# Routing weights of an expert layer: spread by products on TensorE, or stored to DRAM and read back as broadcast rows

## The reference, cut to what matters

```python
def block(x, c, ...):                        # x: (4, 1024, 256), fp32
    sa, ca, ga, sb, cb, gb = modulation(silu(c) @ wmod)
    h = layernorm(x) * (1 + ca) + sa
    x = x + ga * rwkv(h)                     # token mixing, K/V/R products, scan over T, output product
    h = layernorm(x) * (1 + cb) + sb
    x = x + gb * ffn(h)
    return x

def ffn(x):                                  # 8 experts of width 64, the best 2 are taken, one shared of 128
    logits = x @ gate_w.T
    topk_vals, topk_idx = top_k(logits, 2)
    w = softmax(topk_vals)
    comb = zeros(n, 8).at[arange(n)[:, None], topk_idx].add(w)
    g, u = einsum('nh,ehm->enm', x, Wg), einsum('nh,ehm->enm', x, Wu)
    eo = einsum('enm,emh->enh', silu(g) * u, Wd)
    return einsum('ne,enh->nh', comb, eo) + silu(x @ sWg) * (x @ sWu) @ sWd
```

## Time and profile before

| | us |
|---|---|
| time, median of 3 runs | 409.97 (407.69 to 410.45) |
| the profiled execution | 408.2 |
| its span in the trace | 406.3 |
| TensorE busy in the span | 366.6 |
| VectorE busy | 334.6 |
| ScalarE busy | 295.2 |
| GpSimd busy | 44.7 |

### The profile page before, as it was taken

One profiled execution on the slowest core, in us unless ns is written; L12 is line 12 of the kernel. 1 busy time (PEld: TensorE's weight loads), 2 busy tenths in 40 slices (PEclk: granted clock), 3 DMA queues, 4 the chain that ended last, 5 costly groups with the idle time before them and its releaser, 6 DMA issues.

```text
span 406.3 us, 4276 instructions
## 1 busy us (share of the span) xinstructions
PE 366.6 (90%) x1348; PEld 224.8 (55%) x1348; DVE 334.6 (82%) x667; ACT 295.2 (73%) x466; POOL 44.7 (11%) x76
## 2 busy tenths in 40 slices
PE   4892873999999999999999999999999999969985
PEld 4561332756565845675476646574567455725752
DVE  4799989987989898999899898989898988541541
ACT  2699699846997589948994799759985894324332
POOL 4030013001400050002200230005000200010000
PEclk9995795799999999999999999999999999969999
DMA  8900010001000110011000300011001000100011
GB/s 287 268 5 1 0 52 0 0 2 52 0 2 0 52 52 2 0 52 54 0 2 2 103 0 0 2 53 50 2 1 52 2 0 0 52 2 0 0 53 52
DMA packets 15626, 13.27 MB, mean 33 GB/s; under 512 B 4690, under 2 KB 15092, under 8 KB 15604
## 3 DMA queue, kind: packets, MB, share of 16 engines
q1 hardware_dynamic: 15572, 12.99, 10.4%
q10 hardware_dynamic: 32, 0.01, 0.0%
HBM read 8.80 MB, written 4.19 MB: 32 GB/s over the span
## 4 chain that ended last, share of the span: by engine, by line
PE 63%; ACT 22%; DVE 9%; issue 3%; DMA 1%; SPq 0%; DVEq 0%; ACTq 0%
PE mm L737 29%; PE mm L632 10%; PE yo L765 7%; PE yo L650 7%; ACT arg L391 6%; ACT n_xn L326 5%; PE yo L659 3%; ACT arg L417 3%; ACT pool_x L366 2%; ACT h_h L365 2%; ACT kv L374 2%; DVE h_l L979 2%; ACT arg L405 1%; PE cb L749 1%; DVE mixed L879 1%
## 5 line engine op out<-in xcount | busy, mean ns | idle before, releaser
L632 PE MATMUL mm<-mixed,WT 128*128 128x512 f32 x192 | 87.5, 604 | 8.1 <-DVE mixed L879 8.1
L765 PE MATMUL yo<-act,w_dn 128*128 128x512 f32 x160 | 74.1, 613 | 5.4 <-DVE act L1056 5.4
L632 PEld LDWEIGHTS mm<-mixed,WT 128*128 128x128 f32 x192 | 36.3, 193 | 53.4 <-issue 39.6
L737 PE MATMUL mm<-h_h,w_up_h 128*128 128x512 f32 x160 | 55.2, 426 | 4.3 <-DVE h_l L979 4.3
L765 PEld LDWEIGHTS yo<-act,w_dn 128*128 128x128 f32 x160 | 30.8, 197 | 41.9 <-issue 35.6
L737 PE MATMUL mm<-h_l,w_up_h 128*128 128x512 f32 x160 | 51.1, 401 | 0.0
L737 PE MATMUL mm<-h_h,w_up_l 128*128 128x512 f32 x160 | 51.0, 400 | 0.0
L300 POOL TENSOR_TENSOR n_ve<-n_mv,small 128x4 f32<-128x4 f32 x16 | 8.2, 510 | 310.9 <-DVE n_mv L868 310.9
L374 ACT ACTIVATE kv<-mm,cols 128x512 f32<-128x512 f32 x32 | 21.8, 682 | 18.9 <-PE mm L632 18.9
L737 PEld LDWEIGHTS mm<-h_h,w_up_h 128*128 128x128 f32 x160 | 28.4, 192 | 12.6 <-DVE h_l L979 6.4
L737 PEld LDWEIGHTS mm<-h_h,w_up_l 128*128 128x128 f32 x160 | 30.6, 191 | 7.5
(11 more groups left out here) (149 smaller groups left out, 662.6 us busy)
## 6 DMA issues: line engine op xcount, KB each, us to landing
x_in<-in_L_attn_x_dram SPq DMA_DIRECT2D x8, 512.0 KB, 3.5
out_dram<-pool_x SPq DMA_DIRECT2D x5, 512.0 KB, 2.9
pool_x<-in_L_wmod_dram SPq DMA_DIRECT2D x2, 512.0 KB, 4.9
out_dram<-x_third SPq DMA_DIRECT2D x2, 512.0 KB, 2.9
pool_x<-in_L_wmod_dram SPq DMA_DIRECT2D x2, 256.0 KB, 4.0
pool_g<-in_L_ffn_Wg_dram SPq DMA_DIRECT2D x2, 256.0 KB, 5.0
pool_g<-in_L_ffn_Wu_dram SPq DMA_DIRECT2D x2, 256.0 KB, 4.4
w_dn<-in_L_ffn_Wd_dram SPq DMA_DIRECT2D x1, 512.0 KB, 3.9
```

The source lines that it names most:

```text
L632: last = nc.tensor.matmul(mm[PROJECT_BANK[j]][:, :], WT[:, w, kc, oc * P:(oc + 1) * P], mixed[:, w, kc, :], start=(kc == 0), stop=(kc == K ...
L737: last = nc.tensor.matmul(mm[UP_BANK[i]][:, :], w[:, kc, gu, e * P:(e + 1) * P], rhs[:, kc, :], start=(n == 0), stop=(n == 3 * KH - 1))
L765: last = nc.tensor.matmul(yo[oc][:, :], w_dn[:, e, oc * P:(oc + 1) * P], act[:, e, :], start=(e == 0), stop=(e == NB - 1))
```

## The change

`comb` keeps the eight weights as fp32, without the split in a rounded part and a rest, so `route` has 17 instructions. `turn_comb` turns 8 columns and `comb_out` writes `combT`, now 8 partitions by 512 tokens. The four spread products, their matrix `sel` and its preparation at the start on GpSimd and VectorE are gone. SyncE stores `combT` (16 KB) to a DRAM tensor, waits for that store, and issues eight loads for the chunk: for each block i and each half e of the partitions one DRAM row of 512 weights, read 64 times, into `weights`, a new SBUF tile (128 KB for each load, 1 MB for each chunk). In SyncE's list this `spread(n)` stands ahead of store(n-1) and load(n+3). `weigh` reads `weights` in place of PSUM and waits for the two loads of its block. Weigh 1 and 2 are moved in VectorE's list from before and after gate_up 2 and 3 to behind gate_up 4. `comb_out` also waits for the store of the chunk before, and `turn2` waits for combT_done where it waited for act_done.

```diff
@@ -48,6 +48,8 @@
     x_chunks = x.rearrange("b (g t p) h -> (b g) p t h", t=TT, p=P)
     out_chunks = out.rearrange("b (g t p) h -> (b g) p t h", t=TT, p=P)
 
+    comb_dram = nc.dram_tensor("comb_dram", (E, CH), F32, kind="Internal").ap()
+
     with ExitStack() as ctx:
         def sb(name, shape, dt=F32):
             return ctx.enter_context(nc.sbuf_tensor(name, shape, dt))
...
@@ -99,8 +100,9 @@
         h2_l = sb("h2_l", [P, KH, CH], F32R)
         rt = sb("rt", [P, 8, TT, E])
         r1 = sb("r1", [P, 7, TT])
-        comb = sb("comb", [P, TT, 2 * E], F32R)
-        combT = sb("combT", [P, CH], F32R)
+        comb = sb("comb", [P, TT, E])
+        combT = sb("combT", [E, CH])
+        weights = sb("weights", [P, NP, CH])
         lgT = sb("lgT", [2 * E, CH])
 
         pool_x = sb("pool_x", [P, 3 * TT * H])
...
@@ -204,7 +203,8 @@
         comb_done = sem("comb_done")
         comb_turned = sem("comb_turned")
         combT_done = sem("combT_done")
-        comb_mm = sem("comb_mm")
+        comb_stored = sem("comb_stored")
+        spread_in = [sem(f"spread_in{i}") for i in range(NP)]
         up_mm = sem("up_mm")
         silu_done = sem("silu_done")
         prod_done = sem("prod_done")
...
@@ -238,6 +238,19 @@
             def store(c):
                 sp.wait_ge(x2_done, 2 * (c.n + 1))
                 sp.dma_start(out_chunks[c.n], x1[c.n % 3][:, :, :]).then_inc(stored[c.n % 3], 16)
+
+            def spread(c):
+
+
+                sp.wait_ge(combT_done, c.n + 1)
+                sp.dma_start(comb_dram, combT[:, :]).then_inc(comb_stored, 16)
+                sp.wait_ge(comb_stored, 16 * (c.n + 1))
+                for i in range(NP):
+                    wait(sp, act_done, NP * (c.n - 1) + i + 1)
+                    for e in range(2):
+                        sp.dma_start(weights[e * M:(e + 1) * M, i, :],
+                                     comb_dram[2 * i + e:2 * i + e + 1, :].to_broadcast([M, CH])
+                                     ).then_inc(spread_in[i], 16)
 
             load(chunk(0))
             for kc in range(KH):
@@ -260,10 +273,12 @@
             sp.dma_start(w_dn[:, 1:, :], Wd.rearrange("(i e) m h -> (e m) i h", e=2)).then_inc(dn_in, 16)
             sp.dma_start(w_dn[:, 0, :], sWd).then_inc(dn_in, 16)
             load(chunk(2))
-            for n in range(NC - 1):
+            for n in range(NC):
+                spread(chunk(n))
+                if n:
+                    store(chunk(n - 1))
                 if chunk(n + 3):
                     load(chunk(n + 3))
-                store(chunk(n))
             last = chunk(NC - 1)
             for k in range(2):
                 sp.wait_ge(x2_done, 2 * last.n + k + 1)
...
@@ -465,7 +471,8 @@
             @of_chunk
             def comb_out(c):
                 ac.wait_ge(comb_turned, c.n + 1)
-                nc.scalar.activation(combT[0:2 * E, :], cb[0:2 * E, :], ACT.Identity).then_inc(combT_done, 1)
+                wait(ac, comb_stored, 16 * c.n)
+                nc.scalar.activation(combT[:, :], cb[0:E, :], ACT.Identity).then_inc(combT_done, 1)
 
             def split_up(kc):
                 ac.wait_ge(up_in, 8 * 16)
@@ -602,7 +609,7 @@
             def turn2(c):
                 pe.wait_ge(norm2.xn_done, TT * (c.n + 1))
                 if c.n:
-                    pe.wait_ge(act_done, NP * c.n)
+                    pe.wait_ge(combT_done, c.n)
                 else:
                     pe.wait_ge(norm1.h_done, KH * 2)
                 turn(norm2, c, 0, tp)
@@ -695,8 +702,7 @@
             def turn_comb(c):
                 pe.wait_ge(comb_done, c.n + 1)
                 for t in range(TT):
-                    last = nc.tensor.transpose(cb[0:2 * E, t * P:(t + 1) * P], comb[:, t, :].bitcast(F32),
-                                               ident[:, :])
+                    last = nc.tensor.transpose(cb[0:E, t * P:(t + 1) * P], comb[:, t, :], ident[:, :])
                 last.then_inc(comb_turned, 1)
 
             @of_chunk
@@ -740,16 +746,6 @@
                 last.then_inc(up_mm, 1)
 
             @of_chunk
-            def spread_comb(c, e):
-
-                if e == 1:
-                    pe.wait_ge(combT_done, c.n + 1)
-                elif e < 4:
-                    pe.wait_ge(act_done, NP * c.n + e - 1)
-                nc.tensor.matmul(comb_bank[e][:, :], sel[:, e - 1, :], combT[:, :], start=True, stop=True
-                                 ).then_inc(comb_mm, 1)
-
-            @of_chunk
             def down(c, oc):
 
                 if oc == 0:
@@ -795,13 +791,9 @@
                 up(prev, 6)
                 turn_comb(prev)
                 up(prev, 7)
-                spread_comb(prev, 1)
                 up(prev, 8)
                 turn_attn(cur)
-                spread_comb(prev, 2)
                 up(prev, 9)
-                spread_comb(prev, 3)
-                spread_comb(prev, 4)
                 project(nxt, (2, 3, 4, 5))
                 down(prev, 0)
                 turn2(cur)
@@ -1027,13 +1019,8 @@
                         ins = V.tensor_tensor(w1m, m1, wide(w1), ALU.mult)
                     elif n == 15:
                         ins = V.tensor_tensor(w2m, m2, wide(w2), ALU.mult)
-                    elif n == 16:
-                        ins = V.tensor_tensor(pr, w1m, w2m, ALU.add)
-                    elif n == 17:
-                        ins = V.tensor_copy(comb[:, :, 0:E], pr)
                     else:
-                        V.tensor_tensor(comb[:, :, E:2 * E], pr, comb[:, :, 0:E].bitcast(F32), ALU.subtract
-                                        ).then_inc(comb_done, 1)
+                        V.tensor_tensor(comb[:, :, :], w1m, w2m, ALU.add).then_inc(comb_done, 1)
                         return
                     ins.then_inc(route_step, 1)
 
@@ -1051,9 +1038,9 @@
 
             @of_chunk
             def weigh(c, e):
-                ve.wait_ge(comb_mm, NP * c.n + e)
+                ve.wait_ge(spread_in[e - 1], 32 * (c.n + 1))
                 ve.wait_ge(prod_done, NB * c.n + e + 1)
-                nc.vector.tensor_tensor(act[:, e, :], comb_bank[e][:, :], sg[:, e, :], ALU.mult).then_inc(act_done, 1)
+                nc.vector.tensor_tensor(act[:, e, :], weights[:, e - 1, :], sg[:, e, :], ALU.mult).then_inc(act_done, 1)
 
             @of_chunk
             def stats2(c):
@@ -1108,15 +1095,15 @@
                 residual2(before, 0)
                 residual2(before, 1)
                 scan_max(nxt, 1)
-                weigh(prev, 1)
                 gate_up(prev, 2)
                 gate_up(prev, 3)
-                weigh(prev, 2)
                 residual1(cur, 0)
                 residual1(cur, 1)
                 stats2(cur)
                 mix(nxt, 2)
                 gate_up(prev, 4)
+                weigh(prev, 1)
+                weigh(prev, 2)
                 weigh(prev, 3)
                 weigh(prev, 4)
                 stats1(after)
...
```

## The result

| | before | after |
|---|---|---|
| median, us | 410.15 (407.69 to 410.45) | 422.35 (421.1 to 424.7) |
| the profiled execution, us | 408.2 | 424.7 |
| its span, us | 406.3 | 422.9 |
| granted TensorE clock, mean | 0.958 | 0.929 |

The change made the kernel slower: 1.032 times the time of before, 95% interval 1.025 to 1.038. The forecast of 409.4 was wrong, and the time lies above the range. The profiled execution is the longest of the four; the medians lie 12.2 us apart, the two profiles 16.5.

What follows compares the result with a forecast made beforehand. It took a dense loop of TensorE, ScalarE and VectorE to bound the kernel. Steps 1 to 6 at -5.6 us, step 7 at -0.3 and step 8 at +5.3 gave -0.6, so 409.4 us; range 405.8 to 415.5.

Steps and rivals of the forecast that it cites:

- TensorE's microsecond: Steps 1 to 6: four products fewer on TensorE ahead of project save 1.01 us; two steps at -1.0, four at -0.9.
- Rival C: Steps 1 to 6: another wait that the old one hid binds, so nothing is gained; 415.3 us, chance 0.11.
- E: Rival: steps gain 1.5 us each because VectorE is relieved; 405.8 us, chance 0.10.
- The way through DRAM, for the weights: Store lands after 1.5 us, 128 KB loads after 2.45, pairs every 1.1; fourth block hidden with 1.7 us to spare.
- the alternative of 2.0 us: Store of combT to DRAM: the skill's fixed time of about 2.0 us, which would make the last step 0.5 us longer.
- What stands behind spread in SyncE's queue: Load of x, behind eight weight loads and a store, lands at the very limit; 0.1 us charged in steps 2 to 5.
- step 8: Last step, trip through DRAM uncovered: `down` starts 2.4 us later and half clock costs 2.9; sum +5.3 us.
- Step 7: No projections there: residual1 comes 1.5 us sooner, two more weighs follow, weigh 4 ends at 359.8; -0.3 us.
- Rival B: Broadcast weight reads at half rate, pairs every 1.4 us, x 1.1 us too late; 414.8 us, chance 0.22.
- A: The prediction's own sum over all steps: 409.4 us, its own range 407.5 to 412, chance 0.42.
- if the transfers keep up: Condition on weight-load pairs following every two issues, 0.96 us; 1.1 us was taken.
- Rival F: Each small transfer takes 2.5 us more, so weights miss even the middle steps by 2 us; above 420, chance 0.05.

## Why the prediction was wrong

**TensorE's microsecond: right.** -0.9 a step was charged; with x out of the way intervals 2 to 5 come 0.87 to 0.93 us shorter, and interval 6 of the kernel after, which has no load of x, measured -1.09 for -1.0. Rival C, that the gain isn't passed on, and E, that it is 1.5, are both out.

**The way through DRAM, for the weights: right in the middle steps.** The store lands in 1.47 us for 1.5, so the alternative of 2.0 us is out, and no weigh waits in steps 1 to 6. Loads of 128 KB land after 3.0 us for 2.45, inside the bounds.

**"What stands behind spread in SyncE's queue": the step that failed.** Two terms were too small, and the margin was thinner than the error of either. The spacing of issues was taken as 0.48 us, from two loads at the start, and is 0.62 for these: nine issues brought x out 7.1 us after combT, not 5.9. The landing was put at 4.5 us after issue and measured 5.2 (interval 4) to 6.8 (interval 3, with its open 2 us). And stats1 was known to have 0.3 us of room, while x was reckoned by a chain of estimates 10.4 us long. x came 1.9 us (12.3 for 10.4) later than reckoned in interval 4 and 3.5 us in interval 3. The charge was 0.1 us in each of steps 2 to 5 and nothing in step 1; the waits in steps 1 to 5 were 0.94 to 3.62.

**What follows from a wait was not charged.** The text gave half clock to step 8 alone. Behind intervals 2 and 3 the wait for x, passed on to TensorE as some 2 and 4 us idle, was followed by 3 and 7 us at 0.50; behind 4 and 5, with 2.4 and 2.6 us idle, it was not. So intervals 3 and 4 came 3.97 and 3.15 us longer where they should have been 0.9 shorter, by the wait and, as estimated above, 1.5 and 2.3 us of half clock. Intervals 1 to 5 together were forecast at -4.6 and measured +9.3, which is 13.9 of the 14.6 us by which the sum is off without the start (forecast -0.6, measured +14.0).

**Step 7:** +0.19 for -0.3. The last weigh waits 0.76 us for its weights, where the text had it start 0.4 us after they landed; `down` waits 5.49 us for 3.80 and its ten matmuls take 6.78 us for 7.32.

**Step 8: the mechanism right, the sizes off against each other.** +3.83 for +2.4 ahead of `down`: pairs every 1.43 us for 1.1. Clock +1.75 for +2.9. The sum is +5.6 for +5.3. Why less than forecast for the clock: by the windows it fell at about 403.5, while TensorE still idled, and was back at about 410.3, 3.6 us into `down` and not 5.5.

**Rival B** had the right place, the right sign and a pair interval of 1.4 us, as measured. But its price was 5.4 us above A, since it charged each middle step only +0.1, and its cause was not the one at work: the halved rate exists, as the kernels with two loads show, but with eight loads it is hidden behind SyncE's issuing, and taking it away there changed nothing. In the text "if the transfers keep up" was the condition; the issuing itself did not keep up. **Rival F** alone lay above 420, but by weights that miss the middle steps, and no weigh waits there.

## What to carry to other kernels

When work is put into an engine's queue of transfers, cost what is queued behind it first: every issue and every byte ahead of the next load that someone waits for, from rows of the same kind, and if the sum of estimates is far longer than the margin, expect the wait. A wait of some microseconds on a chain through TensorE costs its length and can cost a stretch at half clock after it, as it did behind two of four such waits here. Then give the work only where it has cover (a buffer more, the load sent ahead), and keep the old form where it has none: seven chunks through DRAM and the last one by products was the fastest kernel run here.

## What the runs showed of the hardware that was not expected

- SyncE's time for an issue differs with the partitions and the shape: 0.62 us for 128 KB and for 512 KB onto 64 partitions, neighbouring or not; 0.43 to 0.46 for 128 KB onto 128 partitions; 0.40 for 512 KB onto 128 partitions with 4 KB packets; 0.62 for 256 KB onto 128 partitions from two rows. It differs with what was issued just before as well: the same load of x takes 0.37 us by itself, 0.49 to 0.51 behind the store, and 0.59 where it follows the eight loads directly, in interval 1 (0.43 in the kernel whose eight loads go onto 128 partitions):

```profile
102.45 0.59 SPq L236 DMA_DIRECT2D x_in<-in_L_attn_x_dram  x1
```

- GpSimd's small `n_mr` takes 2.12 us while the four weighs, now with both inputs in SBUF, run on VectorE; with one of them in PSUM it took 0.20. It ends as the weighs do (241.51 plus 2.49). In the two kernels without a late x, intervals 2 to 5 took 42.76 to 42.79 us all the same. GpSimd's timeline before, then after, in the same place of a middle step:

```profile
233.51 0.20 POOL L306 TENSOR_TENSOR n_mr<-n_mv,n_rstd 128x4 f32<-128x4 f32 x1
```

```profile
241.94 2.12 POOL L312 TENSOR_TENSOR n_mr<-n_mv,n_rstd 128x4 f32<-128x4 f32 x1
```

The Trainium skill ("SBUF — State Buffer", section "Who interferes with whom") has this contention for a VectorE instruction with two SBUF inputs, and the trace agrees.

- Eight-row fp32 products ahead of `down` were followed by a granted clock of 0.50 with only 0.78 us idle; 128-row fp32r products in their place were not, with 1.58 us idle (0.50 from about 391.0 to 394.4 in the one, 1.00 in the other). Whether it is the rows, the type or the work between them was not separated.
